# One engine-order rewrite of a byte-tower kernel: group 0 moved through all five queues, and each field's matmuls running over the scales outside

## The chip, the cores and the metric

The kernel runs on one core of a Trainium2 chip. The metric is the device time of one launch in microseconds, the median of several runs. TensorE does the matmuls, VectorE and ScalarE the elementwise work, GpSimd small side calculations, and SyncE issues the stores. Every engine takes its instructions strictly in the order in which the kernel lists them, and waits at an instruction until the semaphores in front of it have the counts that it names.

## The reference, cut to what matters

```python
# 16 sequences of 128 bytes; 64 channels
h  = gelu(conv1d(onehot(x), w1, 7)); h = gelu(conv1d(h, w2, 5)); ctx = sigmoid(conv1d(h, w3, 3))
amps = emb[x] * ctx
for s in range(4):                       # the four scales of the "field"
    z = (positions - center) / (|width| * multiscale_widths[s] + 1e-5)
    basis += exp(-0.5*z*z) * cos(phase + 2*pi*z) * amp_scale * scale_weights[s]**2
h  = einsum('bsp,bsd->bpd', basis, amps)                 # field
h += state_space(layernorm(h))           # a complex linear recurrence, 64 modes, then C
H  = gelu(layernorm(h) @ W1 + b1)        # 256 hidden
probs = softmax(H @ Wg + bg)             # 8 experts, the best one is taken
h += probs[best] * (H @ Wd[best] + bd[best])
```

## The kernel before

The 16 sequences are four groups of four (G = 4, GB = 4). Every step is a small function of the group, and one hand-written list for each engine says in which order these functions are called. There is no planner: the five lists and the semaphores are the schedule.

**The field.** For a group, VectorE makes `z` (L675), the four scales of 512 columns side by side; the phase in turns as integers (`turns`: four instructions on L685, then a mask over all 2048 columns, L690, called the wrap below); ScalarE squares z (`square`, L466), takes exp (`gaussian`, L470), and cos (`cosine`, L476, two halves of two scales each). VectorE multiplies both and the scale's weight (`product`, L732, one instruction for a scale). TensorE sums over the bytes with the amplitudes as weights (`field`, L996, 32 matmuls, two column halves c, four scales s, two row halves r). The amplitudes come from `gates(q)` on VectorE, once for two groups (L713 to L722); `gates(1)` reads them out of the bank that later takes the outputs of the recurrence, so `outputs(0)` waits for both.

**The recurrence.** ScalarE copies the field out (`field_out`, L500), TensorE transposes it (`upright`, L1004), ScalarE copies it to `h_a` (`upright_out`, L504). VectorE takes mean and variance (`moments`, L744 and L747), GpSimd makes 1/std (`inv_std`: variance plus eps on L379, the power on L381 for group 0 and L385 for the others, and for those an offset). Group 0 is normalised by VectorE (L754), the others by ScalarE (L514). TensorE transposes (`turn`, L1015), ScalarE copies (`transposed_out`, L508), TensorE multiplies with B (`inputs_in`, L1025), VectorE makes the drive (`driven`, L765), the scan (L780) and the turn back (L787), and TensorE the outputs (`outputs`, L1042). VectorE adds them to `h_a` (`residual`, L795), and moments, 1/std, normalising and turning come again with n = 1.

**The experts.** `hidden` (L1053, ScalarE: GELU L521 and rounding L532), `gate` (L1063), `logits_back` (L1073), and for each half h of a group `experts_high` (a bias of two matmuls, L1087, then eight on L1080) and `experts_low` (four on L1080); the last half is `experts_in_turn`, the same twelve. VectorE compares the logits (`route`, L802 to L807) and takes the best expert's columns by predicated copies (`pick`, L819, L829). Once the largest logit of all groups is known (`softmax_in`), ScalarE takes exp and VectorE makes the probabilities (`probability`, L838 to L843), once for all groups. Then GpSimd finishes groups 0 to 2 (`finish`, L395 and L399; its first one waits for the probabilities), and VectorE group 3 (`pick_last`, `finish_last`, L848, four times). SyncE issues a store for each of groups 0 to 2 (L279), and behind them, in its order, two for the halves of group 3 (L283).

TensorE's list also has calls of `keep_warm(n, bank)`: n matmuls of zeros (L921) whose result nobody reads, which fill time. Each is 512 columns of bf16.

Of the kernel before, what the change touches and what calls it, by code (L numbers as in the profile page):

```python
# [15 lines left out]
ALU = mybir.AluOpType  # L16
ACT = mybir.ActivationFunctionType
# [54 lines left out]
def tower(nc, x, positions, small, w1, w2, state, wd, bd, out):  # L72
    ctx = ExitStack()
    with ctx:
# [213 lines left out]
        def _(pool):  # L288
# [87 lines left out]
            def inv_std(n, g):  # L376

                pool.wait_ge(s_mv[n], g + 1)
                link(pool.tensor_scalar(var_eps[:, n, g, :], mean_var[:, n, g, :, 1], EPS, None, ALU.add))  # L379
# [3 lines left out]
                else:  # L383
                    pool.tensor_scalar(negated[:, n, g, :], mean_var[:, n, g, :, 0], -1.0, None, ALU.mult)
# [17 lines left out]
            inv_std(0, 1)  # L402
            inv_std(0, 2)
            inv_std(1, 0)
            inv_std(0, 3)
            inv_std(1, 1)
# [6 lines left out]
        def _(act):  # L413
# [137 lines left out]
            act.wait_ge(s_ones_decay, 1)  # L551
            act.activation(decay[:, :, :], decay[:, :, :], ACT.Copy, scale=spar[:, 2:3]).then_inc(s_decay, 1)
            act.wait_ge(ld["state"], 16)
            act.activation(C_part[:, 0, :], C_im, ACT.Copy, scale=spar[:, 4:5]).then_inc(s_C_part, 1)
            act.activation(C_part[:, 1, :], C_im, ACT.Copy, scale=spar[:, 3:4]).then_inc(s_C_part, 1)
            conv2_out(0)
# [5 lines left out]
            cosine(0)  # L562
            cosine(1)
            square(2)
            cosine(2)
            field_out(0)
            load_gelu()
            upright_out(0)
            conv2_out(1)
            load_exp()  # L570
            field_out(1)
            taps_out(1)
            gaussian(2)
            upright_out(1)
            context_out(1)
            square(3)
            transposed_out(0, 0)
            gaussian(3)
            load_sin()
            cosine(3)  # L580
            act.wait_ge(s_gate_pad, 1)
            act.copy(gate_w[:, :, 0:NE], Wg).then_inc(s_gate_w, 1)
            field_out(2)
            normalise(0, 1)
            upright_out(2)
            transposed_out(0, 1)
            load_gelu()
            act.wait_ge(ld["wd"], 16)
            act.copy(wd_high[:, :, :], wd_sb[:, :, :]).then_inc(s_wd_high, 1)
            normalise(0, 2)  # L590
            field_out(3)
            transposed_out(0, 2)
            upright_out(3)
            transposed_out(1, 0)
            hidden(0)
            round_hidden(0)
            normalise(0, 3)
            gate_out(0)
            transposed_out(0, 3)
            normalise(1, 1)  # L600
            transposed_out(1, 1)
            normalise(1, 2)
            hidden(1)
            gate_out(1)
            round_hidden(1)
# [13 lines left out]
        def _(dve):  # L619
# [61 lines left out]
            def turns(g):  # L681
# [7 lines left out]
                link(ins)  # L689
# [47 lines left out]
            def moments(n, g):  # L737
# [8 lines left out]
                for b in range(GB):  # L746
                    ins = dve.bn_aggr(mean_var[:, n, g, b, :], stats[:, n, g, b, :])  # L747
# [527 lines left out]
```

## Time and profile before

| | us |
|---|---|
| median of 3 runs | 111.67 (111.58 to 112.59) |
| the profiled execution, its own time | 111.52 |
| its span in the trace | 109.6 |
| TensorE busy | 100.5 (92%), 83 of the 723 matmuls are of keep_warm |
| VectorE busy | 90.0 (82%) |
| ScalarE busy | 70.8 (65%) |
| GpSimd busy | 51.0 (47%) |
| granted TensorE clock | 1.00 of full speed in every slice |

Times in the trace are microseconds from the start of the span. The time of an execution is some 1.9 us more than its span. An engine that is busy is not always working for the end: TensorE's share holds the fillers.

### The profile page before, as it was taken

How to read it: one execution, taken by the hardware profiler on the slowest of the kernel's cores; microseconds unless marked ns; L12 is line 12 of the kernel's file. 1: busy time of each engine (PE TensorE's matmuls, PEld its weight loads, DVE VectorE, ACT ScalarE, POOL GpSimd, SP SyncE). 2: the span in 40 equal slices, each digit the busy share in tenths (PEclk: the TensorE clock that was granted, in tenths of full speed). 3: DMA queues.
4: the chain of work that ended last, by engine and by line, in shares of the span. 5: the costliest groups of instructions: out<-in, count | busy, mean ns of one | idle time of the engine just before them, and what ended most of it. 6: DMA issues, size and time to landing. Idle time of an engine off the chain costs nothing.

```text
span 109.6 us, 2018 instructions
## 1 busy us (share of the span) xinstructions
PE 100.5 (92%) x723; PEld 64.3 (59%) x723; DVE 90.0 (82%) x230; ACT 70.8 (65%) x126; POOL 51.0 (47%) x101
## 2 busy tenths in 40 slices
PE   5979999999999978869899999999999799999970
PEld 2356785364434576347567477876696476776640
DVE  0359999999999949999999599678999956199892
ACT  4604599999999999999869438454758513551000
POOL 7798998899980007205509426256005000000670
PEclk9999999999999999999999999999999999999999
DMA  3999700000000100000000000000000000000044
GB/s 91 269 233 408 283 0 0 3 0 0 6 0 4 5 0 0 0 0 6 0 0 0 0 6 0 0 0 0 0 0 9 0 0 0 0 0 0 0 96 96
DMA packets 4313, 4.15 MB, mean 38 GB/s; under 512 B 3280, under 2 KB 3536, under 8 KB 4176
## 3 DMA queue, kind: packets, MB, share of 16 engines
q1 hardware_dynamic: 4160, 3.92, 12.5%
q10 hardware_dynamic: 144, 0.12, 0.4%
q8 instruction: 5, 0.08, 0.3%
q14 instruction: 4, 0.03, 0.1%
HBM read 3.50 MB, written 0.52 MB: 37 GB/s over the span
## 4 chain that ended last, share of the span: by engine, by line
PE 42%; ACT 38%; DVE 8%; DMA 4%; issue 4%; POOL 2%; ACTq 0%; DVEq 0%
PE pair L1080 14%; ACT wave L476 8%; PE bank L1042 7%; ACT bell L466 7%; ACT bell L470 5%; ACT L425 5%; DMA ids<-x 4%; DVE pair L819 3%; PE hid_pair L1053 3%; PE pair L951 3%; ACT angle L514 3%; PE pair L921 2%; ACT h L460 2%; PE hid_pair L1063 2%; ACT dist L455 2%
## 5 line engine op out<-in xcount | busy, mean ns | idle before, releaser
L379 POOL TENSOR_SCALAR var_eps<-mean_var 128x4 f32<-128x4 f32 x8 | 3.7, 458 | 33.0 <-DVE mean_var L747 33.0
L819 DVE COPY_PREDICATED pair<-later,pair 128x256 f32<-128x256 int32 (+3 forms) x30 | 12.3, 409 | 5.3 <-PE pair L1080 4.6
L921 PE MATMUL pair<-warm 128*128 128x512 bf16 x53 | 13.3, 380 | 0.0
L732 DVE SCALAR_TENSOR_TENSOR bell<-bell,scale_w,wave 128x512 f32<-128x512 f32 x16 | 10.8, 743 | 0.0
L1080 PE MATMUL pair<-wd_high,H_high 128*128 128x512 f32 x32 | 10.8, 418 | 0.0
L921 PE MATMUL hid_pair<-warm 128*128 128x512 bf16 x30 | 9.0, 455 | 1.3 <-POOL warm L298 1.3
L1080 PE MATMUL pair<-wd_low,H_high 128*128 128x512 f32 x32 | 10.0, 394 | 0.0
L395 POOL TENSOR_TENSOR angle<-picked,prob 128x256 f32<-128x256 f32 x3 | 1.8, 613 | 17.2 <-DVE prob L843 17.2
L521 ACT ACTIVATE bell<-hid_pair,sm 128x512 f32<-128x512 f32 x8 | 5.0, 680 | 7.2 <-PE hid_pair L1053 7.2
L675 DVE TENSOR_TENSOR wave<-dist,inv_width 128x2048 f32<-128x2048 f32 x4 | 9.3, 2356 | 0.0
L965 PE MATMUL pair<-h,w_sb 128*64 128x512 f32 x40 | 9.1, 597 | 0.0
L1080 PE MATMUL pair<-wd_high,H_low 128*128 128x512 f32 x32 | 9.0, 402 | 0.0
L476 ACT ACTIVATE wave<-angle,neg_pi 128x1024 f32<-128x1024 int32 x8 | 8.6, 1138 | 0.1
L385 POOL TENSOR_TENSOR rstd<-var_eps,minus_half 128x4 f32<-128x4 f32 x6 | 8.2, 1366 | 0.0
L685 DVE TENSOR_SCALAR angle<-wave,phase 128x512 int32<-128x512 f32 x16 | 8.0, 561 | 0.0
L921 PEld LDWEIGHTS pair<-warm 128*128 128x128 bf16 x53 | 4.9, 102 | 5.2 <-issue 1.3
L951 PE MATMUL pair<-onehot,w1p 128*128 128x512 f32 x32 | 7.9, 404 | 0.0
L996 PE MATMUL pair<-bell,amps 128*64 128x128 f32 x128 | 7.9, 276 | 0.0
L425 ACT ACT_TABLE_LOAD x6 | 7.7, 1283 | 0.1
L996 PEld LDWEIGHTS pair<-bell,amps 128*64 128x64 f32 x128 | 6.9, 137 | 1.3 <-issue 1.3
L470 ACT ACTIVATE bell<-bell 128x2048 f32<-128x2048 f32 x4 | 7.6, 1920 | 0.0
L466 ACT ACTIVATE bell<-wave 128x2048 f32<-128x2048 f32 x4 | 7.6, 1910 | 0.0
(166 smaller groups left out, 226.1 us busy)
## 6 DMA issues: line engine op xcount, KB each, us to landing
ids<-x SPq DMA_DIRECT2D x2, 512.0 KB, 5.7
posb<-positions SPq DMA_DIRECT2D x1, 768.0 KB, 8.1
wd_sb<-wd SPq DMA_DIRECT2D x1, 512.0 KB, 9.1
out<-angle SPq DMA_DIRECT2D x3, 128.0 KB, 2.0
st_sb<-state SPq DMA_DIRECT2D x1, 328.0 KB, 8.3
w_sb<-w SPq DMA_DIRECT2D x1, 256.0 KB, 6.6
posb<-positions SPq DMA_DIRECT2D x1, 256.0 KB, 6.6
w_sb<-w SPq DMA_DIRECT2D x1, 160.0 KB, 8.0
```

The source lines that it names most:

```text
L425: act.activation(unused[:, k:k + 1], neg_pi[:, :], function)
L466: act.activation(bell[:, g, :], wave[:, g, :], ACT.Square).then_inc(s_square[g], 1)
L470: act.activation(bell[:, g, :], bell[:, g, :], ACT.Exp, scale=-0.5).then_inc(s_bell[g], 1)
L476: act.activation(wave[:, g, part], angle[:, g, part], ACT.Sin, bias=neg_pi[:, 0:1], scale=2.0 * PI_BELOW / TURN).then_inc(s_cos[g], 1)
L675: dve.tensor_tensor(wave[:, g, :].rearrange("p (s t) -> p s t", s=NS), repeat(dist[:, g * GB:(g + 1) * GB, :].rearrange("p b t -> p (b t)" ...
L732: ins = dve.scalar_tensor_tensor(out=bell[:, g, part], in0=bell[:, g, part], scalar=scale_w[:, s:s + 1], in1=wave[:, g, part], op0=ALU.mul ...
L819: return dve.copy_predicated(held[:, :, 0:n, 0, 0:D], repeat(later[:, g, 2 * h + rows.start:2 * h + rows.stop, first:first + n], 3, D), he ...
L921: pe.matmul(bank[free], warm[:, 0:P], warm[:, :], start=True, stop=True)
L951: mm = pe.matmul(bank[g], w1p[part][:, j, :], onehot[:, g * GB:(g + 1) * GB, 2 * j:2 * j + P], start=(part == 0 and j == 0), stop=(part == ...
L965: mm = pe.matmul(bank[2 * q][r * D:(r + 1) * D, :], w2_sb[:, k, :], h1[:, g * GB:(g + 1) * GB, k:k + P], start=(k == 0), stop=(k == K2 - 1))
L996: mm = pe.matmul(bank[g][r * D:(r + 1) * D, c * P:(c + 1) * P], amps[:, g * GB + b, :], bell[:, g, at:at + P], start=(s == 0), stop=(s == ...
L1080: mm = pe.matmul(pair[h][:, jj, :], hidden_part[:, g % 2, k, cols], weights[:, k, :], start=False, stop=last and k == KH - 1)
```

## The change

All five lists keep the same steps with few exceptions, and the order of the steps is another.

- **field** runs the scales outside and the column halves inside. Its first 24 matmuls (scales 0 to 2) need the third scale's product, its last eight the fourth's; `product` takes a range of scales and signals after the third and after the fourth.
- **turns** is cut into `phases` and `wrap`, called apart for group 3.
- For group 0, variance plus eps moves from GpSimd into VectorE's `moments`.
- **TensorE**: one head filler call is gone and one shorter; conv1 runs one group after another; some fillers may wait for a semaphore (`behind`); groups 0's outputs come ahead of field(2); hidden(0) ahead of upright(3); expert parts and `logits_back` stand at other places: `logits_back(3)` was ahead of `experts_low(2, 1)`, and is now behind `experts_high(3, 0)`.
- **ScalarE**: scaling `decay` and filling `gate_w` change places; `transposed_out(0, 0)` ahead of `square(3)`; others as in the diff.
- **VectorE**: all from `wrap(2)` on is reordered; at the end `pick(2, 1)` ahead of `route(3)`, and two `pick_last` ahead of `probability`.
- **GpSimd**: order of `inv_std`.

The diff, cut to its core:

```diff
             def inv_std(n, g):
                 pool.wait_ge(s_mv[n], g + 1)
-                link(pool.tensor_scalar(var_eps[:, n, g, :], mean_var[:, n, g, :, 1], EPS, None, ALU.add))
                 if g == 0:
...
                 else:
+                    link(pool.tensor_scalar(var_eps[:, n, g, :], mean_var[:, n, g, :, 1], EPS, None, ALU.add))
...
             def moments(n, g):
...
+                if g == 0:
+                    link(ins)
+                    ins = dve.tensor_scalar(var_eps[:, n, g, :], mean_var[:, n, g, :, 1], EPS, None, ALU.add)
...
-            def product(g):
-                dve.wait_ge(s_bell[g], 1)
-                for s in range(NS):
+            def product(g, scales):
+                if scales.start == 0:
+                    dve.wait_ge(s_bell[g], 1)
+                for s in scales:
...
-                ins.then_inc(s_prod[g], 1)
+                    if s >= NS - 2:
+                        ins.then_inc(s_prod[g], 1)
...
             def field(g):
                 pe.wait_ge(s_amps, g // 2 + 1)
-                pe.wait_ge(s_prod[g], 1)
-                for c in range(2):
-                    for s in range(NS):
+                for s in range(NS):
+                    if s in (0, NS - 1):
+                        pe.wait_ge(s_prod[g], 1 + s // (NS - 1))
+                    for c in range(2):
...
```

The lists after the change, from the places where they differ (unchanged heads left out):

```python
# ScalarE
C_part x2, gate_w, conv2_out(0), load_exp, gaussian(0), taps_out(0), gaussian(1), context_out(0), cosine(0),
square(2), cosine(1), cosine(2), field_out(0), load_gelu, conv2_out(1), upright_out(0), load_exp, gaussian(2),
field_out(1), decay, taps_out(1), upright_out(1), transposed_out(0,0), square(3), gaussian(3), context_out(1),
load_sin, normalise(0,1), cosine(3), load_gelu, transposed_out(0,1), field_out(2), wd_high, transposed_out(1,0),
upright_out(2), field_out(3), hidden(0), round_hidden(0), upright_out(3), gate_out(0), normalise(0,2),
transposed_out(0,2), normalise(1,1), transposed_out(1,1), normalise(0,3), hidden(1), transposed_out(0,3), ...
# VectorE, behind wrap(2)
input_gain, product(0, 0:2), gates(0), product(0, 2:4), z(3), product(1), phases(3), moments(0,0), wrap(3),
normalise(0,0), product(2, 0:2), moments(0,1), driven(0), scan(0), turn_back(0), product(2, 2), gates(1),
product(2, 3), residual(0), moments(1,0), product(3, 0:3), normalise(1,0), driven(1), product(3, 3), scan(1),
turn_back(1), moments(0,2), weights_rest, residual(1), moments(1,1), split_hidden(0), moments(0,3), route(0),
driven(2), scan(2), turn_back(2), pick(0,0), residual(2), moments(1,2), driven(3), split_hidden(1), scan(3),
turn_back(3), pick(0,1), residual(3), moments(1,3), route(1), pick(1,0), split_hidden(2), pick(1,1), route(2),
pick(2,0), split_hidden(3), pick(2,1), route(3), softmax_in, pick_last(0,0), pick_last(0,1), probability,
finish_last(0,0), finish_last(0,1), pick_last(1,0), finish_last(1,0), pick_last(1,1), finish_last(1,1)
# TensorE (w3 = three fillers), behind context(0), w8, conv2(1), w4
w4 behind cosine(0), field(0), w7, upright(0), w4, field(1), tap(1), w5, upright(1), w2, turn(0,0), w2,
inputs_in(0), context(1), w2, w4 behind driven(0), w5 behind scan(0), outputs(0), turn(0,1), field(2), w2,
inputs_in(1), upright(2), w3 behind 1/std(1,0), turn(1,0), w4, field(3), hidden(0), upright(3), outputs(1),
gate(0), experts_high(0,0), turn(0,2), logits_back(0), experts_low(0,0), inputs_in(2), turn(1,1),
experts_high(0,1), hidden(1), turn(0,3), outputs(2), inputs_in(3), gate(1), experts_high(1,0),
experts_low(0,1), experts_low(1,0), turn(1,2), outputs(3), hidden(2), logits_back(1), experts_high(1,1),
gate(2), experts_low(1,1), logits_back(2), experts_high(2,0), turn(1,3), experts_low(2,0), hidden(3),
experts_high(2,1), gate(3), experts_low(2,1), experts_high(3,0), logits_back(3), experts_low(3,0),
experts_in_turn(3,1)
# GpSimd: inv_std (0,0), (0,1), (1,0), (0,2), (1,1), (0,3), (1,2), (1,3), then finish(0), (1), (2) as before
```

## Rows read from the trace of the kernel before

**Rows 1.** The page, chain that ended last, shares by engine.

```profile
PE 42%; ACT 38%; DVE 8%; DMA 4%; issue 4%; POOL 2%; ACTq 0%; DVEq 0%
```

**Rows 2.** Busy time by window: PE, PEld, DVE, ACT, POOL, then clock, DMA.

```profile
64.00:86.00 22.00, 21.95 (x172) 16.70 (x173) 19.38 (x64) 12.83 (x31) 8.22 (x16) 1.00 0.01 2
```

**Rows 3.** Timeline of VectorE, 30 to 53 us: start, length, instructions, idle before.

```profile
30.20 0.36 DVE L713 TENSOR_SCALAR amp_tmp<-amp_tanh 128x16 f32<-128x16 f32 x1
...
31.65 5.38 DVE L732 SCALAR_TENSOR_TENSOR bell<-bell,scale_w,wave 128x512 f32<-128x512 f32 x8
36.95 2.28 DVE L675 TENSOR_TENSOR wave<-dist,inv_width 128x2048 f32<-128x2048 f32 x1
...
41.61 1.64 DVE L685 TENSOR_SCALAR angle<-wave,phase 128x512 int32<-128x512 f32 x4
43.29 1.23 DVE L690 TENSOR_SCALAR angle<-angle 128x2048 int32<-128x2048 int32 x1
44.59 0.98 DVE L754 TENSOR_SCALAR angle<-h_a,mean_var,rstd 128x64 f32<-128x64 f32 x4
45.49 0.16 DVE L715 SCALAR_TENSOR_TENSOR gain<-ctx_tanh,amp_tmp 128x8 f32<-128x8 f32 x1
...
49.33 0.60 DVE L744 BATCH_NORM_STATS2 stats<-h_a 128x6 f32<-128x64 f32 x4
...
50.26 0.66 DVE L765 TENSOR_TENSOR wave<-bank,turn_tab 128x512 f32<-128x512 f32 x1
...
52.21 1.29 DVE L787 TENSOR_TENSOR wave<-wave,turn_tab 128x512 f32<-128x512 f32 x2
```

**Rows 4.** Timeline of ScalarE, where field 0 is copied out.

```profile
38.52 0.35 ACT L500 COPY angle<-pair 128x256 f32<-128x256 f32 x1
```

**Rows 5.** Timeline of GpSimd, three of the eight powers.

```profile
42.59 1.97 POOL L381 TENSOR_TENSOR rstd<-var_eps,minus_half 128x4 f32<-128x4 f32 x1
...
50.96 2.06 POOL L385 TENSOR_TENSOR rstd<-var_eps,minus_half 128x4 f32<-128x4 f32 x1
...
57.89 1.03 POOL L385 TENSOR_TENSOR rstd<-var_eps,minus_half 128x4 f32<-128x4 f32 x1
```

**Rows 6.** The chain in order of time: start, time on the chain, what.

```profile
53.65 1.97 PE bank L1042 x16
...
56.58 1.13 PE bank L1025 x4
57.71 1.90 PE pair L996 x32
59.61 1.19 PE pair L921 x5
...
64.00 1.06 PE hid_pair L1053 x8
...
92.54 2.95 PE pair L1080 x12
```

**Rows 7.** Timeline of TensorE, its longest idle time behind 64 us.

```profile
87.33 0.44 PE L1015 MATMUL hid_pair<-sm,angle 128*128 128x128 f32 x2 [0.57 <-ACT angle L514]
```

**Rows 8.** Timeline of the end: VectorE, GpSimd, and SyncE's issues (SPq).

```profile
98.57 0.19 DVE L802 TENSOR_TENSOR ladder<-bank,sm 128x32 f32<-128x32 f32 x1
...
99.86 1.48 DVE L819 COPY_PREDICATED pair<-later,pair 128x512 f32<-128x512 int32 x3
...
102.24 0.61 POOL L395 TENSOR_TENSOR angle<-picked,prob 128x256 f32<-128x256 f32 x1 [17.18 <-DVE prob L843]
...
103.66 1.01 DVE L819 COPY_PREDICATED pair<-later,pair 128x256 f32<-128x256 int32 x3
...
105.70 0.73 POOL L399 TENSOR_TENSOR angle<-angle,h_b 128x256 f32<-128x256 f32 x1
...
106.87 1.03 SPq L283 DMA_DIRECT2D out<-angle  x2
107.20 0.28 DVE L848 SCALAR_TENSOR_TENSOR angle<-pair,prob,h_b 128x64 f32<-128x64 f32 x1
```

More of the change, by code:

```diff
@@ L562, in _ @@
             cosine(0)
+            square(2)
             cosine(1)
-            square(2)
             cosine(2)
@@ L853, in _ @@
             z(1)
-            turns(0)
-            turns(1)
-            z(2)
-            turns(2)
+            phases(0)
+            wrap(0)
+            phases(1)
+            wrap(1)
+            z(2)
+            phases(2)
+            wrap(2)
+            input_gain()
+            product(0, range(0, 2))
             gates(0)
-            product(0)
-            product(1)
-            z(3)
+            product(0, range(2, NS))
+            z(3)
+            product(1, range(NS))
+            phases(3)
             moments(0, 0)
-            turns(3)
+            wrap(3)
             normalise(0, 0)
-            gates(1)
-            product(2)
-            input_gain()
+            product(2, range(0, 2))
             moments(0, 1)
@@ L871, in _ @@
             turn_back(0)
-            product(3)
-            moments(0, 2)
+            product(2, range(2, 3))
+            gates(1)
+            product(2, range(3, NS))
             residual(0)
             moments(1, 0)
+            product(3, range(0, 3))
+            normalise(1, 0)
             driven(1)
+            product(3, range(3, NS))
             scan(1)
-            normalise(1, 0)
             turn_back(1)
+            moments(0, 2)
+            weights_rest()
+            residual(1)
+            moments(1, 1)
+            split_hidden(0)
             moments(0, 3)
+            route(0)
             driven(2)
-            weights_rest()
             scan(2)
             turn_back(2)
-            residual(1)
-            moments(1, 1)
+            pick(0, 0)
             residual(2)
             moments(1, 2)
-            split_hidden(0)
-            route(0)
             driven(3)
+            split_hidden(1)
             scan(3)
             turn_back(3)
-            pick(0, 0)
-            split_hidden(1)
+            pick(0, 1)
             residual(3)
@@ L1124, in experts_low @@
                     mm.then_inc(s_exp_mm[h], 1)
-            keep_warm(3, 7)
             embeddings(0)
-            keep_warm(3, 7)
+            keep_warm(2, 7)
             pe.wait_ge(s_onehot, 2)
-            conv1((0, 1))
-            conv1((2, 3))
+            for g in range(G):
+                conv1((g,))
             conv2(0)
@@ L1151, in _ @@
             inputs_in(0)
-            keep_warm(6, 3)
+            context(1)
+            keep_warm(2, 3)
+            keep_warm(4, 3, s_drive)
+            keep_warm(5, 3, s_modes)
+            outputs(0)
+            turn(0, 1)
             field(2)
-            keep_warm(6, 3)
-            outputs(0)
-            upright(2)
-            turn(0, 1)
             keep_warm(2, 3)
             inputs_in(1)
+            upright(2)
+            keep_warm(3, 3, s_rstd[1])
+            turn(1, 0)
+            keep_warm(4, 3)
             field(3)
-            keep_warm(5, 0)
-            turn(0, 2)
+            hidden(0)
             upright(3)
-            keep_warm(6, 0)
-            turn(1, 0)
-            inputs_in(2)
-            hidden(0)
             outputs(1)
```

120 lines of the change are left out of this document (64 added, 56 removed).

## Prediction

> **What bounds the kernel now.** I read the page's chain first: TensorE holds 42% of it and ScalarE 38% [rows 1]. In order of time ScalarE's part lies ahead of 53 us (squares, exps, cosines, table loads) and TensorE's behind it. Next the windows: from 64 to 86 us TensorE is busy 21.95 of 22.00 us [rows 2], with no filler in it, so there every microsecond of needed matmuls counts, wherever in the list it stands. Last the timelines of the end, where three things come within a microsecond of each other: VectorE's last instruction ends at 107.48, GpSimd's last finish at 106.43, and SyncE's last issue at 107.90 [rows 8]. The page's end of the span, 109.6, is some 2.1 us behind the start of that last issue (107.52, VectorE's end plus 0.04). So the time is set by three questions: when hidden(0) starts TensorE's full stretch, how much must be done between it and the last group's logits, and what follows on those logits. I walked the new lists in order with the row's durations; the working below is that walk, cut to the steps that decide.
>
> **Part 1, VectorE from 30.2 to 52 us.** Up to the wrap of group 2 its list is unchanged, and ends at 30.20 [rows 3]. ScalarE comes here about a microsecond earlier (conv1 in single groups, decay's scaling moved away), so field_out(0), at 38.52 before [rows 4], would be near 37.4. That gain is not passed on, since VectorE's own sum is now the longer: input_gain 0.4, four products of group 0 and four of group 1 at 0.67 each, 5.38, gates(0) 1.0 (before 30.20 to 31.65, with GpSimd busy beside it), z(3) 2.28, phases(3) 1.68 [rows 3], in sum 10.7, so 40.95. moments(0,0), 0.93 [rows 3], and its new variance step, for which no row stands: between 0.1 (nothing but a small instruction's issue) and 0.4 (amp_tmp, 30.20); I take 0.2. The end is 42.1, and the GpSimd step that it replaces goes.
>
> **The power of group 0** starts then, together with wrap(3). Before it took 1.97 us, with the wrap beginning 0.7 us after it and both ending together (44.56 and 44.52), where the undisturbed one at 57.89 took 1.03; the one at 50.96 started with the scan and took 2.06 [rows 3, 5]. So it is held up by a VectorE instruction beside it. In the new order I take 2.05, the 50.96 row being nearest: ready at 44.15, normalise(0,0) starts at 44.2. Before: 44.59 [rows 3]. A gain of 0.4 only; the low bound of the power, 1.03, would still leave the wrap's end at 43.35, a further 0.85 gained. The Trainium skill (SBUF — State Buffer, section "Who interferes with whom") says that whichever of the two starts first has the shared port pair for its whole instruction and the other fully blocks. By that rule the wrap, issued first, would make the power end near 44.3, which is the sum by the row within 0.2 us. The 42.59 row speaks against the rule's first half, as it was the earlier starter that got longer.
>
> From 44.2 VectorE has no gap: normalise 0.9, two products 1.35, moments(0,1) 0.93, driven and scan 1.95, turn_back 1.25, third product 0.67, gates(1) 0.80 [rows 3], which is 7.85, so 52.05. outputs(0) needs gates(1) as well as turn_back(0) (both use that bank): it starts at 52.1, not at 50.8 when the turn back is ready. Before: 53.65 [rows 6]. Gain 1.55. ScalarE waits about 1.1 us for turn(0,0) with square(3), gaussian(3), context_out(1) and the cosine behind it. That makes cosine(3) about 1.8 us later than before and takes all its lead, which costs nothing as far as field(3) goes, whose product waits for VectorE anyway.
>
> **Part 2, TensorE from outputs(0) to hidden(0).** Outputs 1.82 (1.97 until the last one's end), turn 0.22, field(2) 1.90, two fillers 0.47, inputs_in(1) 1.0, upright 0.25, three fillers 0.71, turn(1,0) 0.25, four fillers 0.94, field(3) 1.90 (a filler is 1.19/5 = 0.24) [rows 6]: 9.5, and 0.2 for hand-overs (transposed_out(0,1) and normalise(1,0) arrive just then, at about 56.5 and 58.5). hidden(0) at 61.85 against 64.00 [rows 6], a gain of 2.15. The early start of a field's first 24 matmuls is worth nothing here: field(2) stands behind outputs(0), and field(3) behind four fillers that end at 59.8, when its last product is done too. If those fillers were gone it would be worth less than the 0.5 us of eight matmuls.
>
> **Part 3, from hidden(0) to the last route.** Before, 64.00 to 98.57, 34.57 us [rows 6, 8]. Moved into this stretch: experts_high(3,0), 0.32 + 8/12 of 2.95 = 2.29; experts_low(2,1), 4/12 of 2.95 = 0.98; inputs_in(2) 1.0; upright(3) 0.25; turn(0,2) 0.25 [rows 6]. Together 4.77. What goes is idle time: 0.57 at turn(1,3) [rows 7], and small waits, which I put at up to 0.6 more. In the new order I find no large one: turn(1,1) may wait 0.2 for its normalised input, and turn(1,2) and outputs(3) have margins below 0.4. I take 38.55, so route(3) starts at 100.4, **1.83 later than before**. TensorE itself ends near 104.6, earlier than before, as it has only 4.3 us of experts left behind the logits. But the logits of group 3 are what everything at the end hangs on.
>
> **Part 4, the end.** Before, from route(3) to the start of GpSimd's finishes is 98.57 to 102.24, 3.67, with a whole pick of 1.73 in it (99.86 to the next instruction). Now two pick_last, 2 x 1.04, stand there in its place: 4.02. GpSimd's three finishes take 102.24 to 106.43, 4.19 [rows 8], at either place. So probabilities arrive at 104.42 and the third finish ends at 108.6. VectorE, with only two picks and four finishes behind the probabilities, ends near 107.5, earlier than that. SyncE's order now matters: the store of group 2 waits for GpSimd, and both stores of group 3 stand behind it. Issues cost about 0.41 each when they follow on one another (two in 0.85, from 106.87 and 1.03 with a wait in it [rows 8]). Last issue: 108.6 + 0.03 + 0.41 + 0.41 = 109.45, against 107.52: 1.93 later. The span becomes 111.5, the run 111.52 + 1.9 = 113.4. The profiled run lies 0.15 below the median, so the median becomes 113.5.
>
> Costs taken at nothing: the ones in the head (an earlier conv1 is hidden by VectorE's unchanged list to 30.2; uncovered in neither direction), the filler calls behind a semaphore (48 against 45 behind the head, all but nine of them in time in which TensorE waits anyway; those nine, 2.1 us, are in part 2's sum). An idle TensorE could bring the granted clock down; it is 1.00 throughout before, and its longest new wait is some 1.3 us ahead of outputs(0), so I leave it out, with up to 1 us in the upper end.
>
> **The rivals.** (a) *The collisions between GpSimd and VectorE go away.* Not slower. In the trace the phases of group 2 took 2.80 us, 1.1 more than group 3's 1.68, and the power 1 us more than its undisturbed row. If the other order parts them, 30.20 becomes 29.1 and the power is ready with the wrap: 1.1 + 0.85 earlier at outputs(0), and as all of part 2 to 4 is in sequence, the end too: 111.55. It decides from 0.8 us on that the result is within 1%. For it: these two are the largest excesses over the plain rows. Against: all of VectorE and GpSimd up to 30.2 keeps its order.
> (b) *GpSimd's finishes shrink.* If with VectorE quieter they took 0.9 each (0.61 + 0.73 less what the other engine costs), VectorE would end last, at 107.5, as before: 111.7. Against: the three ran at the same length whatever stood beside them.
> (c) *Late hand-overs in the full stretch.* Each of the thin margins in part 3 broken once, 0.4 us each at four places, or the clock lowered for a few microseconds: 114.9.
> (d) *Faster.* Part 3's stretch has less in it than I count, or outputs(0) gets forward to 50.8 as well as (a): 2 + 1.3 = 3.3 earlier than the forecast, 110.2. It would take route(3) to start before 97.4.
> That the change doesn't do what it says is true of its named part, the 24 matmuls, and is in the sum at zero.
>
> **How the numbers follow.** This kernel's measurement can tell about 1% from no change, 1.1 us. Forecast 113.5, chance 0.52, own spread 112.8 to 114.3. (a) 0.15, (b) 0.10, both within 1%; (c) 0.14; (d) 0.09. Slower by over 1%: 0.66; within: 0.25; faster: 0.09. The range leaves out (d) and the far end of (c): 111.4 to 114.8.
>
> **What the profile after would show.** normalise(0,0) at about 44.2; the power of group 0 near 2 us; outputs(0) at 52.1 right behind gates(1); hidden(0) near 61.9; TensorE without idle time behind it, and route(3) starting near 100.4, behind experts_high(3,0); the first finish at 104.4; the chain ending over GpSimd L399 and SyncE, with three issues in a row behind it. I am wrong if route(3) starts before 98.6, if GpSimd is not last, or if the store of group 2 is issued before VectorE is through.

## The result, and the profile after

The changed kernel took 116.23 us (median of four runs, 115.0 to 120.45) against 112.12 in the same runs of the kernel before; ratio 1.033, 95% interval 1.022 to 1.044. It is slower, as forecast, but above the stated range of 111.4 to 114.8. The executions of the changed kernel differ by 5 us, and the profiled one is the slowest, 120.45 us with a span of 117.9; the other three had spans of 113.2, 114.4 and 114.4. In all that follows, medians and ranges hold every execution, while ratios and their intervals leave out those that took over 1.5% longer than the fastest of the same kernel.

The page of the profiled execution, the granted clock in 40 slices of 2.95 us, and the chain by engine [rows 1]:

```profile
PEclk9996799999999999996569999999999999999996
...
PE 48%; DVE 21%; ACT 9%; POOL 9%; issue 5%; DMA 4%; POOLq 1%; DVEq 0%; ACTq 0%
```

Before, the clock row was 9 in all slices. Now it falls twice inside the work, at 9 to 15 us and at 53 to 62 us. The chain has moved from ScalarE (38% before) to VectorE and GpSimd, as the sum of part 1 and the end of part 4 had it. The windows, in the columns of rows 2:

```profile
52.00:54.00 2.00, 0.69 (x4) 0.10 (x1) 1.97 (x5) 1.99 (x5) 0.00 (x0) 0.95 0.00 0
54.00:56.00 2.00, 1.77 (x9) 1.80 (x10) 0.78 (x2) 2.00 (x5) 0.00 (x0) 0.57 0.04 8
56.00:58.00 2.00, 2.00 (x11) 1.74 (x10) 0.24 (x1) 1.98 (x2) 0.00 (x0) 0.50 0.00 0
58.00:60.00 2.00, 2.00 (x19) 1.93 (x20) 1.90 (x11) 0.56 (x3) 0.49 (x1) 0.50 0.00 0
60.00:62.00 2.00, 1.84 (x20) 1.67 (x18) 2.00 (x6) 0.43 (x2) 0.96 (x1) 0.70 0.00 0
```

The first number with "(x" is TensorE. From 52 to 54 us it is busy 0.69 of 2 us; then come some 7 us at or near 0.50, which is 1.2 of 2.4 GHz. TensorE's timeline of the same stretch, with what answers to rows 6:

```profile
51.39 1.30 PE L942 MATMUL pair<-warm 128*128 128x512 bf16 x5 [0.20 <-DVE wave L788]
54.23 0.50 PE L1064 MATMUL bank<-Cb_re,wave 128*128 128x64 f32 x2 [1.54 <-DVE amps L725]
54.52 0.64 PE L1064 MATMUL bank<-neg_Cb_im,wave 128*128 128x64 f32 x2
...
58.07 3.44 PE L1018 MATMUL pair<-bell,amps 128*64 128x128 f32 x32
...
66.86 1.17 PE L1075 MATMUL hid_pair<-angle,st_sb 64*128 64x256 f32 x8
```

The wait is the one that part 1 of the prediction placed there: outputs(0) is released by the amplitudes of gates(1) (L725), after 1.54 us of idle time. Its sixteen matmuls then take 3.28 us (54.23 to 57.51) in place of 1.81, and field(2) 3.44 in place of 1.97. The power of group 0, and what answers to rows 3, 5 and 8:

```profile
44.09 1.95 POOL L380 TENSOR_TENSOR rstd<-var_eps,minus_half 128x4 f32<-128x4 f32 x1 [12.46 <-DVE var_eps L755]
...
110.66 0.61 POOL L395 TENSOR_TENSOR angle<-picked,prob 128x256 f32<-128x256 f32 x1 [17.37 <-DVE prob L851]
...
114.09 0.72 POOL L399 TENSOR_TENSOR angle<-angle,h_b 128x256 f32<-128x256 f32 x1
```
```profile
43.84 0.17 DVE L755 TENSOR_SCALAR var_eps<-mean_var 128x4 f32<-128x4 f32 x1
43.92 1.22 DVE L693 TENSOR_SCALAR angle<-angle 128x2048 int32<-128x2048 int32 x1
...
46.08 0.98 DVE L762 TENSOR_SCALAR angle<-h_a,mean_var,rstd 128x64 f32<-128x64 f32 x4 [0.94 <-POOL rstd L380]
...
106.60 0.19 DVE L810 TENSOR_TENSOR ladder<-bank,sm 128x32 f32<-128x32 f32 x1 [0.66 <-PE bank L1095]
```
```profile
112.10 3.11 SPq L279 DMA_DIRECT2D out<-angle  x3
115.25 1.03 SPq L283 DMA_DIRECT2D out<-angle  x2
```

The power again takes 1.95 us, beside the wrap, and VectorE waits 0.94 for it. GpSimd's third finish ends at 114.81, VectorE's last instruction at 113.58, and the three last stores are issued in a row behind GpSimd. None of the three signs of being wrong came: route(3) did not start before 98.6, GpSimd is last, and the store of group 2 is issued behind VectorE's end. So the mechanism of the end is the forecast one, and a clock that I had left out is on top of it.

### The profile page after: what moved, and what is told of

It reads as the page before. It is cut to its first block, busy times and chain, and to the rows that moved or that the text cites. A ratio compares the mean times of both kernels' runs of the same rounds, so it can differ in the third digit from the quotient of the medians.

```text
span 117.9 us, 2013 instructions
## 1 busy us (share of the span) xinstructions
PE 105.6 (90%) x717; PEld 69.2 (59%) x722; DVE 90.6 (77%) x232; ACT 71.2 (60%) x126; POOL 47.7 (40%) x99
## 2 busy tenths in 40 slices
DMA packets 4313, 4.15 MB, mean 35 GB/s; under 512 B 3280, under 2 KB 3536, under 8 KB 4176
## 4 chain that ended last, share of the span: by engine, by line
PE 48%; DVE 21%; ACT 9%; POOL 9%; issue 5%; DMA 4%; POOLq 1%; DVEq 0%; ACTq 0%
PE pair L1102 11%; PE pair L972 8%; PE bank L1064 7%; DVE bell L736 6%; PE pair L1018 5%; DMA ids<-x 4%; PE pair L986 4%; PE hid_pair L1075 4%; ACT angle L514 2%; ACT bell L470 2%; POOL rstd L385 2%; DVE stats L749 2%; POOL rstd L380 2%; PE pair L942 2%; DVE pair L827 2%
## 5 line engine op out<-in xcount | busy, mean ns | idle before, releaser
L942 PE MATMUL pair<-warm 128*128 128x512 bf16 x53 | 14.0, 390 | 0.5 <-DVE wave L788 0.2
L383 POOL TENSOR_SCALAR var_eps<-mean_var 128x4 f32<-128x4 f32 x6 | 2.7, 452 | 24.0 <-DVE mean_var L752 23.9
L380 POOL TENSOR_TENSOR rstd<-var_eps,minus_half 128x4 f32<-128x4 f32 x2 | 3.4, 1699 | 20.6 <-DVE var_eps L755 20.6
L942 PE MATMUL hid_pair<-warm 128*128 128x512 bf16 x24 | 8.3, 513 | 1.5 <-POOL warm L298 1.3
L1018 PE MATMUL pair<-bell,amps 128*64 128x128 f32 x128 | 9.5, 311 | 0.0
L1018 PEld LDWEIGHTS pair<-bell,amps 128*64 128x64 f32 x128 | 8.5, 159 | 1.7 <-issue 1.7
L972 PE MATMUL pair<-onehot,w1p 128*128 128x512 f32 x32 | 9.3, 455 | 0.0
L972 PEld LDWEIGHTS pair<-onehot,w1p 128*128 128x128 f32 x32 | 7.1, 224 | 2.3 <-DVE onehot L648 0.5
L1064 PE MATMUL bank<-Cb_re,wave 128*128 128x64 f32 x32 | 6.9, 302 | 1.5 <-DVE amps L725 1.5
L362 POOL TENSOR_TENSOR turn_tmp<-waves 128x18 f32<-128x18 f32 (+6 forms) x7 | 8.0, 1142 | 0.7 <-POOL waves L351 0.2
```

The source lines that it names most:

```text
L362: link(pool.tensor_tensor(moved, pairs, turn, ALU.mult))
L942: pe.matmul(bank[free], warm[:, 0:P], warm[:, :], start=True, stop=True)
L972: mm = pe.matmul(bank[g], w1p[part][:, j, :], onehot[:, g * GB:(g + 1) * GB, 2 * j:2 * j + P], start=(part == 0 and j == 0), stop=(part == ...
L1018: mm = pe.matmul(bank[g][r * D:(r + 1) * D, c * P:(c + 1) * P], amps[:, g * GB + b, :], bell[:, g, at:at + P], start=(s == 0 and c == 0), ...
L1064: mm = pe.matmul(layer_bank[:, b * D:(b + 1) * D], turned[:, g, r, j * P:(j + 1) * P], c, start=(r == 0), stop=(r == 1))
```

## The experiments

Two questions: how much is the clock, and is the rest what the prediction says it is? Theory A: the open wait ahead of outputs(0) costs the clock. Theory B: the head's missing fillers do. Theory C: the end hangs on the last logits and on what was put behind them. The kernel before was timed beside each of them, with medians of 111.6 to 111.9.

**e1, the wait filled.**

```diff
-            keep_warm(5, 3, s_modes)
+            keep_warm(12, 3, s_modes)
```

> The changed kernel with seven more fillers (12 for 5) in TensorE's wait ahead of outputs(0), where its profile shows 1.54 us of idle time and, right behind it, a granted clock of 0.50 from 55 to 60 us. Theory A (this wait costs the clock, and the slow stretch is what the prediction missed): no slow stretch behind 54 us, outputs(0) 1.8 us long in place of 3.5, field(2) 1.9 in place of 3.4, and about 3 us less than the changed kernel's profiled run; against the changed kernel's median of 116.2 about 1.5 to 2.5 us less, as its other runs were less disturbed. Theory B (the clock follows the fillers taken from the head): the slow stretch behind 54 us stays and the time is within 0.5 us of 116.2. Theory C (the clock is noise of single executions): likewise no steady difference.

Measured: 115.68 us (115.16 to 116.57), ratio 1.036 (1.032 to 1.041). TensorE's timeline of its profiled execution (115.27 us, span 113.2), no slow stretch:

```profile
49.69 2.76 PE L942 MATMUL pair<-warm 128*128 128x512 bf16 x12 [0.23 <-DVE wave L788]
52.52 0.41 PE L1064 MATMUL bank<-Cb_re,wave 128*128 128x64 f32 x2
...
54.65 1.97 PE L1018 MATMUL pair<-bell,amps 128*64 128x128 f32 x32
...
62.27 1.13 PE L1075 MATMUL hid_pair<-angle,st_sb 64*128 64x256 f32 x8
...
71.09 0.44 PE L1037 MATMUL hid_pair<-sm,angle 128*128 128x128 f32 x2 [0.51 <-ACT angle L514]
```

outputs(0) takes 1.81 us and field(2) 1.97, and hidden(0) starts 4.6 us earlier than in the changed kernel's profile (the head, too, was at full clock in this one). But the median moved by 0.5 us only, where I had expected 1.5 to 2.5: the wait's drop lies in the upper part of the spread. Three of the six executions have spans of 113.2 to 113.4, the other three 114.2 to 114.8 with mean clocks of 0.971 to 0.975, so something still slows half of them. With the head filled as well (e3, below) none is like that, which points at the head; no execution of this kind was profiled here, so that is not shown. And the profiled one, 115.3 us with the clock at 1.00 until TensorE was done, is still 1.8 above the forecast, so the prediction missed something besides.

**e2, the head filled, the wait left open.**

```diff
+            keep_warm(3, 7)
             embeddings(0)
-            keep_warm(2, 7)
+            keep_warm(3, 7)
```

> The changed kernel with the head's fillers as before (three ahead of embeddings(0), three behind, for none and two). Its profile shows conv1 taking 9.25 us, with a granted clock below 0.8 near 9 to 13 us, against 7.5 before, and ScalarE waiting 1.24 us for conv2(0). Theory B: conv1 back to 7.5 us and the whole about 1 us faster than the changed kernel, since VectorE waited 1.39 us for ScalarE's cosine behind it. Theory A: the head gives at most 1 us and the slow stretch behind 54 us stays, 115.2 to 116.2.

Measured: 118.4 us (115.38 to 118.83), ratio 1.039 (1.032 to 1.046). Five of the six executions were at 116.7 or above, so that with its head filled the kernel is 2.2 us slower at the median, where neither theory allowed more than 116.2. Four of them have spans of 116.5 to 117.0, longer than that of the profiled one (115.0); why is open. In its profile the head ran at a clock of 1.00, and the drop behind the wait was there all the same, this time in the middle of outputs(0):

```profile
53.15 0.41 PE L1064 MATMUL bank<-Cb_re,wave 128*128 128x64 f32 x2 [1.58 <-DVE amps L725]
...
54.51 0.49 PE L1064 MATMUL bank<-Cb_re,wave 128*128 128x64 f32 x2
54.79 0.64 PE L1064 MATMUL bank<-neg_Cb_im,wave 128*128 128x64 f32 x2
...
55.78 3.06 PE L1018 MATMUL pair<-bell,amps 128*64 128x128 f32 x32
```

So it is not the head's fillers (theory B) that this drop hangs on. The other drop, the one in the head, is a different matter: it is missing here, as in e1's profile.

**e3, both filled**, the edits of e1 and e2 together.

```diff
+            keep_warm(3, 7)
             embeddings(0)
-            keep_warm(2, 7)
+            keep_warm(3, 7)
...
-            keep_warm(5, 3, s_modes)
+            keep_warm(12, 3, s_modes)
```

> The changed kernel with both fillings. If the clock is all that the prediction missed, the profile shows 1.00 throughout and the time is the predicted 113.5, within 0.6. If something else was missed, it stays above 114.3. hidden(0) would start at 61.9, route(3) at 100.4.

Measured: 115.59 us (115.56 to 117.15), ratio 1.037 (1.032 to 1.042); five of six executions between 115.56 and 115.64, and all six spans 113.8. Beside e2, whose only difference is the seven fillers, that is 2.8 us less at the median, and spans of 113.8 in place of 113.6 to 117.0. Theory A stands for the drop behind the wait. The mean clocks of e3 are 0.978 to 0.992 all the same, without a loss: in the profiled execution the clock is 1.00 as long as TensorE works, and falls behind its last matmul (106.63), while GpSimd and the stores finish:

```profile
108.00:110.00 2.00, 0.00 (x0) 0.00 (x0) 1.33 (x5) 0.00 (x0) 1.84 (x4) 1.00 0.29 66
110.00:112.00 2.00, 0.00 (x0) 0.00 (x0) 0.00 (x0) 0.00 (x0) 0.67 (x1) 0.62 0.47 107
```

The head's fillers have a price of their own. ScalarE waits for conv2(0), where in e1 it does not, and everything behind it is 0.6 us later than in e1 (hidden(0) at 62.88 against 62.27, spans 113.8 against 113.2):

```profile
22.75 0.69 ACT L482 ACTIVATE h<-pair,sm 128x512 f32<-128x512 f32 x1 [0.79 <-PE pair L986]
```

So of the 2.1 us that e3 lies above 113.5, 0.6 are these fillers and none is the clock's; e1's faster executions are the changed kernel at full clock.

**e4, both filled, and the end's order nearly as before.**

```diff
             experts_low(2, 1)
-            experts_high(3, 0)
             logits_back(3, 4)
+            experts_high(3, 0)
...
-            pick(2, 1)
             route(3)
             softmax_in()
-            for jj in range(2):
-                pick_last(0, jj)
+            pick(2, 1)
             probability()
...
```

> As the run with both fillings, and with the tail's order of before: logits_back(3) ahead of experts_high(3,0) in place of behind it, and on VectorE route(3) and softmax_in ahead of pick(2,1), and the probabilities ahead of all pick_last. By the prediction's parts 3 and 4 route(3) starts 2.3 us earlier than in the run with both fillings and GpSimd's finishes end 2.6 earlier; VectorE's last picks take over as the end, so that the whole is 1.6 to 2.3 us faster: 111.2 to 111.9. If the end did not hang on the logits but on TensorE's last matmul, the difference is below 0.5.

Measured: 113.17 us (112.73 to 114.02), ratio 1.013 (1.009 to 1.017), 2.4 less than e3; I had expected 1.6 to 2.3 less, and 111.2 to 111.9 from a start of 113.5 that was itself too low. Timeline of the end (VectorE's route(3) and last instruction, GpSimd's first finish):

```profile
100.01 0.19 DVE L810 TENSOR_TENSOR ladder<-bank,sm 128x32 f32<-128x32 f32 x1 [0.96 <-PE bank L1092]
...
108.42 0.28 DVE L856 SCALAR_TENSOR_TENSOR angle<-pair,prob,h_b 128x64 f32<-128x64 f32 x1
```
```profile
103.67 0.61 POOL L395 TENSOR_TENSOR angle<-picked,prob 128x256 f32<-128x256 f32 x1 [14.54 <-DVE prob L851]
```

VectorE is last again, at 108.70, as before the change. One difference from the old end is left: `logits_back(3)` still stands behind `experts_low(2, 1)`, 0.98 us of TensorE, and was ahead of it in the kernel before.

**e5, the kernel before with the new end only.** VectorE's last lines as in the change, and `logits_back(3)` moved behind both `experts_low(2, 1)` and `experts_high(3, 0)`, where e4 moves it over the second alone. By the prediction's prices that is 3.27 us against 2.29.

> The kernel before with only the end of the change: logits_back(3) behind experts_high(3,0), and VectorE's last list of the change (pick(2,1), route(3), softmax_in, two pick_last, probabilities). Theory C (parts 3 and 4 of the prediction: the end hangs on the last logits, then the probabilities, GpSimd's three finishes and SyncE's three issues in a row): TensorE's last matmul stays at 106.0, route(3) moves from 98.6 to 101.8, and the time rises by 3.0 us, to 114.7. Rival (TensorE's last matmul or VectorE's last picks set the end): less than 0.7 us more, 111.7 to 112.4.

Measured: 115.22 us (114.93 to 116.58; I had expected 114.7), ratio 1.033 (1.027 to 1.039): the whole loss of the change at full clock, from its last steps alone. The profiled execution has a span of 113.2, as e1's has. Its timeline:

```profile
101.83 0.19 DVE L802 TENSOR_TENSOR ladder<-bank,sm 128x32 f32<-128x32 f32 x1 [0.67 <-PE bank L1076]
...
105.39 0.61 PE L1083 MATMUL pair<-wd_high,H_low 128*128 128x512 f32 x2
...
105.88 0.61 POOL L395 TENSOR_TENSOR angle<-picked,prob 128x256 f32<-128x256 f32 x1 [20.86 <-DVE prob L843]
...
109.31 0.72 POOL L399 TENSOR_TENSOR angle<-angle,h_b 128x256 f32<-128x256 f32 x1
110.47 1.03 SPq L283 DMA_DIRECT2D out<-angle  x2
```

TensorE ends at 106.00, where it ended before, and the run is 3.6 us longer. What can be seen is theory C step by step: route(3) at 101.83 against 98.57 [rows 8], the finishes from 105.88 (4.05 behind it; predicted 4.02) to 110.03 (4.15; predicted 4.19), and the last two stores behind them. The rival, that TensorE's or VectorE's last work sets the end, falls. Of the 3.6 us, 3.26 are the later route(3), TensorE's list, and 0.38 the longer way from it to the finishes, VectorE's (4.05 against 3.67); this split is read from the trace, as e5 changes both lists at once.

**e6, the kernel before with the named part only**: the loops of `field` and the two signals of `product`.

> The kernel before with only the named part: field over the scales outside, its first 24 matmuls behind the third product. The prediction puts it at zero where something else holds field up: fillers stand ahead of three of the four fields. 111.7 within 0.4. If the early start reached the end, up to 0.5 us less; if the changing of halves cost TensorE something, 0.1 to 0.5 more.

Measured: 111.70 us (111.34 to 113.72), ratio 1.0004 (0.999 to 1.002). A field takes 1.97 us as before. The part that the change is named after is worth nothing by itself, in either direction.

**e7 and e8, where it is worth something.** Both are e4 without the fillers ahead of field(3); e8 also waits for the fourth product at the field's start.

```diff
             turn(1, 0)
-            keep_warm(4, 3)
             field(3)
```
```diff
# e8, besides
-                    if s in (0, NS - 1):
-                        pe.wait_ge(s_prod[g], 1 + s // (NS - 1))
+                    if s == 0:
+                        pe.wait_ge(s_prod[g], 2)
```

> As the run with both fillings and the old tail, without the four fillers ahead of field(3). In that run's trace turn(1,0) ends at 59.96, the third product of group 3 is done at 58.65 and the fourth at 60.80. With the fillers gone field(3) starts at 60.0, its last eight matmuls at 61.4, hidden(0) 0.9 us earlier, and the whole is 0.6 to 0.9 us faster: 112.3 to 112.6 against 113.2. If those fillers kept the clock up, a slow stretch follows and it is slower than 113.2.

> As the run without the fillers ahead of field(3), with field waiting for the fourth product at its start, as before the change. Theory: without the fillers the early start is worth what it saves: field(3) begins at 60.9 and not at 60.0, so this is 0.8 us slower than its pair, near 113.1. Rival (the early start is worth nothing here either, since VectorE's scan and turn back for outputs(1) are late next): within 0.3 of its pair.

Measured: e7 112.82 us (112.48 to 113.17; ratio 1.010, 1.007 to 1.013), e8 114.15 (113.4 to 116.2; 1.020, 1.014 to 1.026). In the profiled executions, field(3) of e7 and of e8:

```profile
60.18 1.97 PE L1015 MATMUL pair<-bell,amps 128*64 128x128 f32 x32
```
```profile
61.40 1.97 PE L1015 MATMUL pair<-bell,amps 128*64 128x128 f32 x32 [0.91 <-DVE bell L736]
```

The spans are 110.8 and 111.5, 0.7 us apart with 0.91 of wait; 0.24 of that is there already at turn(1,0), ahead of field(3) (59.81 and 60.05), so the early start saves 0.5 to 0.7 us where no filler covers it. e8's median is farther off because three of its six executions had a lower clock, 0.970 to 0.983. That its new wait of 0.9 us did this is not shown: the profiled execution has the wait and a clock of 1.00 behind it. e7 against e4 gives 0.35 us where I expected 0.6 to 0.9; hidden(0) came forward by 0.73 us (62.08 against 62.81), but TensorE's last pair of matmuls only from 105.91 to 105.70, so most of it went into waits of the full stretch.

**e9, the front shortened.** e7 with gates(1) ahead of the third product of group 2, transposed_out(0,1) ahead of a table load, and fillers fitted to the waits:

```diff
-            product(2, range(2, 3))
             gates(1)
-            product(2, range(3, NS))
+            product(2, range(2, NS))
...
-            load_gelu()
             transposed_out(0, 1)
+            load_gelu()
...
-            keep_warm(12, 3, s_modes)
+            keep_warm(9, 3, s_modes)
...
-            keep_warm(2, 3)
             inputs_in(1)
...
-            keep_warm(3, 3, s_rstd[1])
+            keep_warm(5, 3)
```

> As the run without the fillers ahead of field(3), and the front shortened where its trace shows waits: gates(1) ahead of the third product of group 2 (outputs(0) waited for it), three fewer fillers ahead of outputs(0), transposed_out(0,1) ahead of the table load for gelu, the two fillers ahead of inputs_in(1) gone, and five in place of three ahead of turn(1,0), not held by the semaphore. outputs(0) 0.67 us earlier (52.4), hidden(0) 0.6 to 0.9 us earlier (near 61.3), the whole 112.0 to 112.3. If the front does not reach the end because of waits behind hidden(0), it stays at 112.8.

Measured: 111.93 us (111.69 to 112.19), ratio 0.9995 (0.996 to 1.003). hidden(0) starts at 61.41, 1.4 us earlier than in e4 and 2.6 earlier than before the change, and the whole, somewhat better than the 112.0 to 112.3 that I expected, is just level with the kernel before.

**e10, and the last logits earlier than in either kernel.**

```diff
-            logits_back(2, 4)
-            experts_high(2, 0)
             turn(1, 3)
-            experts_low(2, 0)
+            logits_back(2, 4)
             hidden(3)
-            experts_high(2, 1)
+            experts_high(2, 0)
             gate(3)
-            experts_low(2, 1)
+            experts_low(2, 0)
             logits_back(3, 4)
+            experts_high(2, 1)
+            experts_low(2, 1)
```

> The shortened front, and the last logits earlier than in either kernel: turn(1,3) and hidden(3) ahead of experts_high(2,0), gate(3) behind it, logits_back(3) ahead of experts_high(2,1), on VectorE route(3) and softmax_in ahead of pick(2,0), on ScalarE normalise(1,3) ahead of gate_out(2). If the end hangs on logits, probabilities and what follows on them, this frees it to follow TensorE's last matmul by 1.4 us plus the store: 110.9 to 111.5, at or below the kernel before. If the picks on VectorE are late next, 111.6 to 112.3.

Measured: 112.52 us (111.38 to 115.14), ratio 1.0015 (0.997 to 1.006). Six of its twelve executions have spans of 109.5 to 109.7 and one 110.6, against 109.9 to 110.2 of e9 and 109.4 to 109.9 of most of the kernel before. The gain over e9 is below what can be told, and no version that I ran beats the kernel before clearly. The other five had spans of 111.1 to 112.6 and a clock of 0.970 to 0.985; in the profiled one the drop was in the head. Its window there:

```profile
10.00:12.00 2.00, 2.00 (x26) 1.42 (x25) 1.93 (x9) 0.84 (x4) 1.77 (x5) 0.50 1.05 404
```

The head of e10 is that of e3 and e9, in whose profiles no such drop was seen, so the head can fall with its fillers in place. The kernel before, timed beside it, had eight of 29 executions with spans of 111.2 to 112.9 and clocks of 0.970 to 0.986. What starts the drop there stays open.

**e11, the kernel before with a wait opened** at the same place.

```diff
             field(2)
-            keep_warm(6, 3)
             outputs(0)
```

> The kernel before without the six fillers between field(2) and outputs(0), so that TensorE stands idle for 1.9 us there (0.4 before). Theory A (an open wait of this length ahead of outputs costs the clock): a stretch at half clock behind 53.6 us in most executions, outputs(0) up to 3.5 us long in place of 1.8, and 0.5 to 3 us more than 111.6. Rival (it was not the wait but the whole of the changed stretch, with its small matmuls): 111.6 within 0.3 and a clock of 1.00.

Measured: 112.74 us at the median of twelve (111.5 to 114.86), the clock between 0.970 and 0.985 in ten of them. Four of the ten have spans of 111.4 to 112.9, as eight of 29 of the kernel before have, and may be drops in the head like that of e10. Six have spans of 110.5 to 110.8 with clocks of 0.978 to 0.985, which none of the 29 has. Timeline and a window of the profiled one, one of the six:

```profile
53.84 0.41 PE L1042 MATMUL bank<-Cb_re,wave 128*128 128x64 f32 x2 [1.82 <-DVE wave L787]
...
54.53 0.40 PE L1042 MATMUL bank<-neg_Cb_im,wave 128*128 128x64 f32 x2
54.75 0.61 PE L1042 MATMUL bank<-Cb_re,wave 128*128 128x64 f32 x2
```
```profile
54.00:56.00 2.00, 2.00 (x14) 2.00 (x14) 2.00 (x4) 1.22 (x4) 0.00 (x0) 0.69 0.00 0
```

Six fillers fewer and nothing else, and the clock halves behind the wait in the kernel before too. The rival, that it takes the whole changed stretch, falls. The ratio, 1.002 (0.997 to 1.006), does not tell it from the kernel before; what shows the loss is the six executions and the profile.

**e12, the changed kernel once more**, without an edit.

> The changed kernel once more, unaltered, for the spread of its executions and a second profile. Theory A (the open wait ahead of outputs(0) drops the clock, for a length that differs by execution): most executions have a mean clock below 0.99, and the profile again shows outputs(0) near 3.5 us, with field(2) behind it in part or all at half clock; median 115.5 to 118.5. If the first profile was an exception, outputs(0) takes 1.8 us and the executions lie within 0.5 of 115.6, as in the run with both fillings.

Measured: 116.46 us (115.05 to 120.34), ratio 1.034 (1.025 to 1.042), spans from 113.3 to 118.5 and clocks from 0.924 to 0.987. Its profile, of an execution with a span of 117.4, again has the slow stretch behind the wait, and the one in the head; the first was no exception.

## Why the prediction was wrong

The direction and its cause were right; the size was not, for two reasons. Of the 2.7 us between 113.5 and 116.2, 1.7 are the sum at full clock and the rest is the clock. The sum alone was enough to leave the range: the changed kernel's fastest executions, 115.0, are above 114.8 too.

**The clock, left out.** The step that failed is the last paragraph of part 4: "its longest new wait is some 1.3 us ahead of outputs(0), so I leave it out, with up to 1 us in the upper end". The wait was there, at 1.54 us, and it was enough. With the wait open and the head filled (e2) the spans go from 113.6 to 117.0; with both filled (e3) they are all 113.8. With the head as in the change, the spans go up to 118.5 with the wait open, and to 114.8 with it filled (e1). In the profiled execution the drop cost 1.5 us in outputs(0) and 1.5 in field(2), and the one in the head 1.4 in conv1 (9.26 us, against 7.83 in e1). At the median the clock costs 0.9 to 1.4 us (116.2 and 116.5 against 115.0 to 115.3 of the fastest executions of the changed kernel and of e1). Which drop that is, the runs do not show. Of the changed kernel's twelve executions three have spans of 113.2 to 113.7, five 114.2 to 114.9, and four 117.3 to 118.5. The two that were profiled are of the last group and have both drops; the middle group is as long as the slower half of e1, where the wait is filled, so its loss is likely the head's. The Trainium skill (TensorE: Matmul & The Clock Gate, section "HAM oscillation — how this bites in real kernels") ties the lower clock to idle time of TensorE; the trace agrees in kind, and the drop came behind a shorter wait than the page's advice would lead one to expect.

**The sum at full clock, 1.7 us too small** (a span of 113.2 against 111.5). Against e1, which is the changed kernel at full clock:

| step | predicted | e1 |
|---|---|---|
| outputs(0) | 52.1 | 52.52 |
| hidden(0) | 61.85 | 62.27 |
| from there to route(3) | 38.55 | 39.59 |
| to the first finish | 4.02 | 4.05 |
| three finishes | 4.19 | 4.15 |
| third finish to the end of the span | 2.9 | 3.14 |

```profile
28.01 1.36 DVE L693 TENSOR_SCALAR angle<-angle 128x2048 int32<-128x2048 int32 x1
29.29 0.83 DVE L780 SCALAR_TENSOR_TENSOR Cb_re<-st_sb,spar,C_part 128x64 f32<-128x64 f32 x1
...
101.86 0.19 DVE L810 TENSOR_TENSOR ladder<-bank,sm 128x32 f32<-128x32 f32 x1 [0.66 <-PE bank L1095]
```
```profile
105.91 0.61 POOL L395 TENSOR_TENSOR angle<-picked,prob 128x256 f32<-128x256 f32 x1 [17.30 <-DVE prob L851]
...
109.34 0.72 POOL L399 TENSOR_TENSOR angle<-angle,h_b 128x256 f32<-128x256 f32 x1
```

- Part 1 came within 0.4 us, in part by luck: VectorE's sum leads, the power takes its 2 us beside the wrap, and gates(1) releases outputs(0). But the unchanged list, which I let end at 30.20, ended at 29.29 in e1, where the phases of group 2 took 2.34 us; `input_gain`, which I put at 0.4, then took 1.04, and VectorE waited another 0.20 for a cosine. In e1 outputs(0) is another 0.1 late by the filler that I put in too many.
- Part 2 was right: 9.75 against 9.7.
- Part 3 is the term that was mis-sized, by 1.0 us. The step that failed is "What goes is idle time: 0.57 at turn(1,3) [rows 7], and small waits, which I put at up to 0.6 more": I took off 0.57 and some of up to 0.6 of idle time, 0.8 net. TensorE's windows from hidden(0) to route(3), before and in e1, show that there was less to take off:

```profile
64.00:98.57 34.57, 33.94 (x241) 24.83 (x242) 27.18 (x83) 18.32 (x41) 8.22 (x16) 1.00 0.00 1
62.27:101.86 39.59, 38.81 (x265) 28.07 (x264) 30.73 (x98) 20.89 (x48) 10.81 (x20) 1.00 0.00 1
```

  Before, TensorE was idle for 0.63 us in all. With the 4.77 of work that moved in, its busy time alone comes to 38.71, which is more than the 38.55 that I gave the whole stretch (38.81 measured). And the idle time did not go: it is 0.78 in e1, 0.51 of it at turn(1,1) and 0.27 at turn(1,2). The wait at turn(1,1) is at the end of a chain that starts where outputs(1) ends, read from the trace and not tried: VectorE's residual and moments (65.55 to 67.02), GpSimd's 2.46 us, as long as before the change (2.45), and ScalarE's normalising to 71.03. TensorE's work in between ends 0.51 us too early.

```profile
67.11 0.58 POOL L383 TENSOR_SCALAR var_eps<-mean_var 128x4 f32<-128x4 f32 x1 [0.58 <-DVE mean_var L752]
```
```profile
69.60 1.43 ACT L514 ACTIVATE angle<-h_b,offset,rstd 128x64 f32<-128x64 f32 x4 [0.52 <-POOL offset L386]
```

- Part 4 was right up to the third finish, and e5 shows it alone: 3.6 us from the last lines of the lists. Its issues were 0.2 short: I read the 1.03 us of the last two as having a wait in it and took 0.41 each, and they took 1.03 again in e1 and e5, where all their inputs are ready.
- TensorE ended at 106.03 in e1, as before the change, and not at 104.6: parts 1 and 3 again.
- The named part at zero: right (e6), and right in its condition, that fillers cover it. I put its worth without them below 0.5 us; e7 and e8 say 0.5 to 0.7.

Of the rivals, (b) did not happen: the finishes took 4.15. By the prediction's own issue times it would not have been level with 111.7 either, but near 112.1. Of (a), one half was there in e1, VectorE's list ahead by 0.9 us at the wrap, and was lost again behind it; in the changed kernel's two profiles the phases of group 2 took 2.66 us (2.80 before). The power took 1.95 in all of them. (c) named late hand-overs and the clock, at 114.9 (four times 0.4 above 113.5 would be 115.1); both came, and together they were more.

So the account of the 4.5 us (116.2 against 111.7): the new end costs 3.6 by itself (e5). The new front brings hidden(0) forward by 1.7 us in e1, but inputs_in(2), upright(3) and turn(0,2), 1.5 us, are then done behind it instead of ahead, and nothing reaches the end: e1 and e5 have the same span, 113.2. The clock adds 0.9 to 1.4 at the median. e4 fits this: its 111.0, less 0.6 for the head's fillers and 0.98 for `experts_low(2, 1)`, is 109.4, by this estimate level with the 109.6 before. That these terms add up so is read from separate kernels, not from one.

## What to carry to other kernels

An early milestone is no gain if needed work was moved behind it: sum a full engine's stretch to its last dependent result, not to its start, and take no more idle time off than its window shows, since a new order brings waits of its own. Work out what each order change does to the last result that something serial hangs on (here logits, then probabilities, then 4 us of GpSimd, then three store issues in one queue), since the engine that ends its own list earlier may be the wrong one to look at. When a filler is cut or a wait is lengthened, price the slower clock behind it, and look at the spread of executions, not only at the median. A mean clock below 1.00 alone is no loss: look where in the timeline it fell.

## What the runs showed of the hardware

- A wait of 1.54 to 1.82 us on TensorE was followed by half clock in four profiled executions, for 7 us in the changed kernel's two and 3.5 us in e2 and e11, and in the kernels where fillers held it to 0.2 no profile has it there. The drop comes with the first matmuls behind the wait, or 0.9 (e11) and 1.5 us (e2) into the work. Waits of 1.04 us (at L1025 in the kernel before) and 0.91 (e8, at field(3)) were followed by none in their profiles.
- When TensorE has finished its list and the others have not, the clock falls too: in e3 it is 1.00 until 110 us and 0.62 from 110 to 112, with TensorE done at 106.6. That alone gives mean clocks of 0.978 to 0.992 in executions of one and the same span.
- GpSimd's power on four columns took 1.02 to 1.06 us in most places and 1.95 to 1.97 beside VectorE's wrap, whether it began 0.7 us before the wrap (kernel before) or 0.2 behind it (after), while the wrap kept its 1.22 to 1.23: the wait is on GpSimd's side in both orders. Beside VectorE's scan it took 2.06 where it began 0.01 behind the scan (kernel before), and 1.06 where it began 0.11 ahead of it (e1):

```profile
48.29 1.06 POOL L385 TENSOR_TENSOR rstd<-var_eps,minus_half 128x4 f32<-128x4 f32 x1
```
```profile
48.40 1.23 DVE L788 TENSOR_TENSOR_SCAN wave<-decay,wave 128x512 f32<-128x512 f32 x1
```

- In the changed kernel's first profile from 7 us on the clock stood at 0.95 and not at 1.00 outside the two drops, and conv2's first twenty matmuls took 4.71 us in place of 4.52; in the second profile it was 1.00 and 4.52.
